# Moving the last batches' comparisons and row additions ahead, and summing both in one loop, in a graph layer kernel

## The reference

```python
h = maximum(layernorm(x), 0)
ea = edge_attr @ W_edge.T + b_edge
msg = relu(h[src] + ea)                                 # one row of 96 for each edge
aggr = segment_sum(msg, dst, num_segments=6250)
z = relu(((1 + eps) * h + aggr) @ W1.T + b1)
return x + z @ W2.T + b2
```

## Time and profile before

| | |
|---|---|
| median of the runs | 1079.86 us |
| span of the profiled execution | 1239.1 us |
| PE busy | 628.9 us, 51% |
| DVE busy | 518.5 us, 42% |
| ACT busy | 193.0 us, 16% |
| POOL busy | 785.9 us, 63% |
| chain that ended last | 56% another core or an unknown queue, 23% DVE, 8% issue, 8% DVE's queue, 3% PE |

### The profile page before, as it was taken

One profiled execution on the slowest core, in us unless ns is written; L12 is line 12 of the kernel. 1 busy time (PEld: TensorE's weight loads), 2 busy tenths in 40 slices (PEclk: granted clock), 3 DMA queues, 4 the chain that ended last, 5 costly groups with the idle time before them and its releaser, 6 DMA issues.

```text
span 1239.1 us, 9124 instructions
## 1 busy us (share of the span) xinstructions
PE 628.9 (51%) x2786; PEld 515.6 (42%) x2786; DVE 518.5 (42%) x658; ACT 193.0 (16%) x233; POOL 785.9 (63%) x838
## 2 busy tenths in 40 slices
PE   2226544455554454555554555444555545554568
PEld 2215434344433334444444444343444434443456
DVE  6645344444433333354344333333343444333373
ACT  5102111111111111111111111111111111111114
POOL 6756666666666666666666666666666666666540
PEclk9999666665656665565665656655556565565668
DMA  8513222333222223333333332222222333232212
GB/s 217 145 33 94 66 64 67 74 85 74 67 67 67 68 67 75 72 73 75 74 93 95 76 74 66 67 67 67 64 66 68 74 88 72 68 67 61 49 29 78
DMA packets 51183, 93.30 MB, mean 75 GB/s; under 512 B 17722, under 2 KB 20443, under 8 KB 51136
## 3 DMA queue, kind: packets, MB, share of 16 engines
q0 software_dynamic: 26592, 40.85, 16.3%
q1 hardware_dynamic: 24390, 51.63, 15.2%
q10 hardware_dynamic: 154, 0.24, 0.1%
HBM read 87.85 MB, written 4.80 MB: 75 GB/s over the span
## 4 chain that ended last, share of the span: by engine, by line
another core or an unknown queue 56%; DVE 23%; issue 8%; DVEq 8%; PE 3%; DMA 1%; ACT 0%; SPq 0%; ACTq 0%
DVE edge_ps L854 7%; DVE edge_ps L865 5%; DVE msg_parts L879 4%; DVEq L768 3%; DVE acc L759 2%; DVEq L770 2%; DVE acc L849 1%; PE edge_ps L601 1%; DVEq L762 1%; DVE stats L639 1%; PE edge_ps L462 1%; DVEq L795 1%; DVE select L705 1%; DVEq L783 1%
## 5 line engine op out<-in xcount | busy, mean ns | idle before, releaser
L352 POOL DMA_INDIRECT gathered<-h_table,src_all x810 | 764.5, 944 | 396.4 <-issue 234.7
L462 PE MATMUL edge_ps<-w_edge,edge_in 97*128 97x96 f32 x1660 | 403.6, 392 | 521.4 <-issue 517.1
L462 PEld LDWEIGHTS edge_ps<-w_edge,edge_in 97*128 97x128 f32 x1660 | 361.8, 302 | 565.0 <-issue 564.1
L787 DVE TENSOR_REDUCE sums<-agg_ps 128x192 f32<-128x576 f32 x41 | 31.0, 757 | 590.4 <-remote 590.4
L424 ACT ACTIVATE msg_parts<-edge_ps 128x960 bf16<-128x960 f32 (+1 forms) x83 | 79.2, 957 | 970.1 <-DVE edge_ps L865 704.4
L543 PE MATMUL agg_ps<-msg_parts,select 128*128 128x288 bf16 x816 | 167.9, 386 | 6.4 <-issue 6.4
L705 DVE TENSOR_TENSOR select<-const_ps,dst_rel 128x2560 bf16<-128x2560 f32 (+1 forms) x43 | 120.8, 2812 | 34.8 <-issue 28.5
L543 PEld LDWEIGHTS agg_ps<-msg_parts,select 128*128 128x128 bf16 x816 | 109.4, 134 | 60.9 <-issue 8.1
L865 DVE TENSOR_TENSOR edge_ps<-edge_ps,gathered 128x960 f32<-128x960 f32 (+1 forms) x83 | 90.9, 1141 | 47.9 <-remote 42.8
L854 DVE SCALAR_TENSOR_TENSOR edge_ps<-edge_ps,msg_parts 128x960 f32<-128x960 f32 (+1 forms) x83 | 91.1, 1144 | 0.3 <-issue 0.3
L879 DVE TENSOR_TENSOR msg_parts<-edge_ps,msg_parts 128x960 bf16<-128x960 f32 (+1 forms) x83 | 90.8, 1136 | 0.3 <-issue 0.3
(11 more groups left out here) (73 smaller groups left out, 143.1 us busy)
## 6 DMA issues: line engine op xcount, KB each, us to landing
edge_in<-edge_t_dram SPq DMA_DIRECT2D x165, 240.0 KB
gathered<-h_table,src_all POOLq DMA_INDIRECT x810
x_all<-x_dram SPq DMA_DIRECT2D x5, 420.0 KB
h_all<-x_dram SPq DMA_DIRECT2D x10, 210.0 KB
out_dram<-h_all SPq DMA_DIRECT2D x10, 210.0 KB
h_table<-h_all SPq DMA_DIRECT2D x3, 420.0 KB
h_table<-h_all SPq DMA_DIRECT2D x1, 630.0 KB
dst_by_row<-dst_rows_dram SPq DMA_DIRECT2D x1, 480.0 KB, 4.2
```

What stands on the lines that cost most here:

```text
L352: nc.gpsimd.indirect_dma_start(out=gathered[c % SLOTS][:, at:at + D], out_offset=None, in_=table, in_offset=bass.IndirectOffsetOnAxis(ap=s ...
L462: mm = pe.matmul(edge_bank(c, g)[:, (k - k0) * D:(k - k0 + 1) * D], edge_in[c % SLOTS][:, k * EDGE_TILE:(k + 1) * EDGE_TILE], w_edge[:], s ...
```

## The change

Late comparisons: both `make_late_select` calls move from behind the loop over batches into its last pass (`c == END`), ahead of the sums of the batch before `END`, with the loads of `END`'s bounds. Row additions: `add_rows(LAST)` moves ahead of `sum_windows(END)` on DVE, so both late row additions stand ahead of it. On PE, the edge features of `LAST` move ahead of the window of `END`. The late sums of both batches are made in one loop, whose length is the larger of their spans (a third small reduction in the set-up makes it). The turn of `END`'s sums and its addition into `acc` come last on both engines.

```diff
--- before.py
+++ after.py
...
@@ -524,17 +524,18 @@
                     pe.reg_add(window, window, 1)
                     pe.reg_add(selects, window, 1)
 
-            def sum_late_windows(c):
-                span = pe.value_load(bounds_i[0:1, 2 * BOUND_ROWS + c:2 * BOUND_ROWS + c + 1], min_val=0, max_val=N - 1)
-                pe.wait_ge(late_relu_done, c - LATE + 1)
-                if c == LAST:
-                    pe.wait_ge(tail_relu_done, 1)
+            def sum_late_windows():
+                span = pe.value_load(bounds_i[0:1, 2 * BOUND_ROWS + JOINT:2 * BOUND_ROWS + JOINT + 1], min_val=0, max_val=N - 1)
                 with pe.Fori(0, span + 1, WINDOW):
-                    this_select = pe.snap(late[c])
-                    pe.wait_ge(late_selected[c], this_select)
-                    sum_rows(c).then_inc(late_summed, 1)
-                    pe.reg_add(window, window, 1)
-                    pe.reg_add(late[c], late[c], 1)
+                    this_select = pe.snap(late)
+                    for c in (LATE, LAST):
+                        pe.wait_ge(late_relu_done, c - LATE + 1)
+                        if c == LAST:
+                            pe.wait_ge(tail_relu_done, 1)
+                        pe.wait_ge(late_selected[c], this_select)
+                        sum_rows(c).then_inc(late_summed, 1)
+                    pe.reg_add(window, window, 2)
+                    pe.reg_add(late, late, 1)
 
             def sum_parts(c):
                 for s in range(SIDES):
@@ -559,23 +560,25 @@
             for c in range(BATCHES):
                 if 0 <= c - BASE_FROM < BASES:
                     turn_base(c - BASE_FROM)
-                if c == LAST:
+                if c == LATE:
+                    edge_features(LAST)
+                    sum_windows(END)
+                elif c == LAST:
                     turned_window = pe.snap(window)
+                    sum_late_windows()
                     pe.wait_ge(sums_made, turned_window)
                     pe.wait_ge(acc_summed, turned_window)
                     turn_sums().then_inc(agg_done, 1)
                     pe.reg_add(window, window, 1)
-                    sum_late_windows(LATE)
-                elif c >= 1:
-                    sum_windows(c - 1)
-                if c + 1 < BATCHES:
+                else:
+                    if c >= 1:
+                        sum_windows(c - 1)
                     if c == 0:
                         pe.wait_ge(ones_copied, 1)
                     edge_features(c + 1)
-            sum_late_windows(LAST)
             all_summed = pe.snap(window)
             all_selects = pe.snap(selects)
-            all_late = {c: pe.snap(late[c]) for c in (LATE, LAST)}
+            all_late = pe.snap(late)
 
             def hidden_sums(c):
                 if c >= 2:
...
@@ -716,6 +719,8 @@
                                                 bounds_f[0:1, 0:BOUND_ROWS], ALU.subtract))
                 sides_of = span_f[:, 0:BOUND_ROWS].rearrange("p (c s) -> p c s", s=SIDES)
                 ordered(nc.vector.tensor_reduce(span_f[:, BOUND_ROWS:BOUND_ROWS + BOUND_ROWS // 2], sides_of, AX.X, ALU.max))
+                ordered(nc.vector.tensor_reduce(span_f[:, BOUND_ROWS + JOINT:BOUND_ROWS + JOINT + 1],
+                                                span_f[:, BOUND_ROWS + LATE:BOUND_ROWS + LAST + 1], AX.X, ALU.max))
                 nc.vector.tensor_copy(bounds_i[:, 2 * BOUND_ROWS:2 * BOUND_ROWS + BOUND_ROWS // 2],
                                       span_f[:, BOUND_ROWS:BOUND_ROWS + BOUND_ROWS // 2]).then_inc(bounds_ready, 1)
 
@@ -764,11 +769,15 @@
                 dve.reg_mul(node[s], node[s], below)
                 dve.reg_add(node[s], node[s], N)
 
+            def load_firsts(c):
+                return [dve.value_load(bounds_i[0:1, SIDES * c + s:SIDES * c + s + 1], min_val=0, max_val=N - 1)
+                        for s in range(SIDES)]
+
+            def load_span(c):
+                return dve.value_load(bounds_i[0:1, 2 * BOUND_ROWS + c:2 * BOUND_ROWS + c + 1], min_val=0, max_val=N - 1)
+
             def load_bounds(c):
-                firsts = [dve.value_load(bounds_i[0:1, SIDES * c + s:SIDES * c + s + 1], min_val=0, max_val=N - 1)
-                          for s in range(SIDES)]
-                span = dve.value_load(bounds_i[0:1, 2 * BOUND_ROWS + c:2 * BOUND_ROWS + c + 1], min_val=0, max_val=N - 1)
-                return firsts, span
+                return load_firsts(c), load_span(c)
 
             def lower_offsets(at, tiles):
                 return nc.vector.tensor_scalar(dst_rel[:, at:at + tiles], dst_rel[:, at:at + tiles], float(-WINDOW), None,
@@ -808,31 +817,31 @@
                     dst_rel[:, first_tile[c]:first_tile[c] + tiles].unsqueeze(2).broadcast_to((128, tiles, WINDOW)),
                     ALU.is_equal).then_inc(late_selected[c], 1)
 
-            def sum_late_windows(c, firsts, span):
-                at, tiles = first_tile[c], tiles_of[c] + (c == LAST)
+            def sum_late_windows(firsts, span):
                 with dve.Fori(0, span + 1, WINDOW) as done:
-                    this_window, this_late = dve.snap(window), dve.snap(late)
-                    dve.reg_add(window, window, 1)
-                    dve.reg_add(offsets, offsets, 1)
-                    dve.reg_add(late, late, 1)
-                    next_window, lowered = dve.snap(window), dve.snap(offsets)
-                    for s in range(SIDES):
-                        next_node(s, firsts[s], done)
-                    cols = [cols_of(s) for s in range(SIDES)]
-                    dve.wait_ge(late_summed, this_late)
-                    dve.wait_ge(acc_summed, this_window)
-                    add_sums(0, cols[0], late_sums(c, 0)).then_inc(side_summed, 1)
-                    lower_offsets(at, tiles).then_inc(offsets_made, 1)
-                    dve.wait_ge(side_summed, this_window)
-                    add_sums(1, cols[1], late_sums(c, 1)).then_inc(acc_summed, 1)
+                    for c in (LATE, LAST):
+                        this_window, this_late = dve.snap(window), dve.snap(late)
+                        dve.reg_add(window, window, 1)
+                        dve.reg_add(offsets, offsets, 1)
+                        dve.reg_add(late, late, 1)
+                        for s in range(SIDES):
+                            next_node(s, firsts[c][s], done)
+                        cols = [cols_of(s) for s in range(SIDES)]
+                        dve.wait_ge(late_summed, this_late)
+                        dve.wait_ge(acc_summed, this_window)
+                        add_sums(0, cols[0], late_sums(c, 0)).then_inc(side_summed, 1)
+                        lower_offsets(first_tile[c], tiles_of[c] + (c == LAST)).then_inc(offsets_made, 1)
+                        dve.wait_ge(side_summed, this_window)
+                        add_sums(1, cols[1], late_sums(c, 1)).then_inc(acc_summed, 1)
+                    lowered, next_window = dve.snap(offsets), dve.snap(window)
                     dve.wait_ge(offsets_made, lowered)
                     dve.wait_ge(acc_summed, next_window)
-                    make_late_select(c)
-
-            def add_turned():
+                    for c in (LATE, LAST):
+                        make_late_select(c)
+
+            def add_turned(turned, cols):
                 this_window = dve.snap(window)
-                cols = [cols_of(s) for s in range(SIDES)]
-                dve.wait_ge(agg_done, this_window)
+                dve.wait_ge(agg_done, turned)
                 dve.wait_ge(acc_summed, this_window)
                 add_sums(0, cols[0], turned_of(0)).then_inc(side_summed, 1)
                 dve.wait_ge(side_summed, this_window)
@@ -890,6 +899,10 @@
                     dve.wait_ge(tail_edge_done, 1)
                     dve.wait_ge(tail_gather_in, 16)
                     nc.vector.tensor_tensor(tail_gathered[:], tail_ps, tail_gathered[:], ALU.add).then_inc(tail_added, 1)
+                if c == END:
+                    make_late_select(LATE)
+                    make_late_select(LAST)
+                    end_bounds, joint_span = load_bounds(END), load_span(JOINT)
                 if c >= 1:
                     if 0 < c - BASE_FROM <= BASES:
                         dve.wait_ge(base_put, c - BASE_FROM)
@@ -903,15 +916,13 @@
                     dve.wait_ge(h_by_act, ACT_PARTS)
                     dve.wait_ge(h_by_dve, DVE_PARTS)
                     nc.vector.memset(hidden[D:D + 1, :], 1.0).then_inc(hidden_ones_set, 1)
-            make_late_select(LATE)
-            make_late_select(LAST)
-            end_bounds, late_bounds, last_bounds = (load_bounds(c) for c in (END, LATE, LAST))
             add_rows(LATE)
+            add_rows(LAST)
             sum_windows(END, *end_bounds)
-            add_rows(LAST)
-            add_turned()
-            sum_late_windows(LATE, *late_bounds)
-            sum_late_windows(LAST, *last_bounds)
```

(14 more changed lines are left out.)

## The result

The changed kernel took 1088.16 us (median of 5, 1087.33 to 1088.60), the kernel before 1079.23 us (5 runs): a ratio of 1.0077, 95% interval 1.0066 to 1.0088. In a later set of its own it was 1.0070 (1.0057 to 1.0084). The forecast was 1084.7 us, 4.8 us slower, with 1087.3 as the upper end: the direction is right, and the time lies 0.9 us above the range.

The account below looks back on a forecast made before the run. The pace of POOL's gathers, 1.25 us each, was taken as the bound. The MLP start moves from G + L + 6.8 to G + L + 11.6: 4.8 us on the median 1079.86 gives 1084.7 us, range 1078.3 to 1087.3.

Parts of the forecast that it names:

- Timed runs don't have the late PE of the profile: Steady part: POOL hardly waits in timed runs, so 161.8 us of its profiled waits go, leaving a span of 1077.3 us.
- The 8.0 us that this left over: Whole kernel: median less 1071.9 us (profiled span without POOL's waits and 5.4 us of end), around the span or unaccounted for.
- G: End of the last gather's issue on POOL, 1196.41 us in the prediction's profile; the end's times count from it.
- first rival: Kernel's end: PE's answers late in timed runs too; changed kernel 0.5 us faster, 1079.3 us; chance 0.25.
- The chain behind `LAST`'s add: DVE's end in the changed kernel: from `LAST`'s add, waiting for the very last gather, to the MLP, 11.6 us.
- Late compares ahead are free: DVE before `END-1`'s sums: two compares, 2.21 us, moved ahead cost nothing and gain nothing, as the next stop is a landing.
- The end of before: Kernel before, last gather's issue end to the MLP: G + L + 6.8, against G + L + 11.6 after the change.
- L: Time from the end of a gather's issue to its data being usable, taken as 2.0 us, ends 1.7 and 4.2.
- L stands once in both figures and drops out: MLP start in both kernels: each figure holds L once, so it leaves the difference of 4.8 us.
- Clock: MLP's first block on PE: a longer PE gap may lower its clock, 2.2 us more, 1086.9 us; chance 0.07.
- G is the same in both: Last gather's issue: the change doesn't delay it; taken as nothing.
- the set-up's delay: Set-up on DVE: the added joint-bound reduction could delay the end, bounds nothing and 1.4 us, taken as nothing.

Follow-up runs that it names:

- r1_before: The kernel before, unchanged, run again for a profile in which POOL doesn't wait: ratio 0.9999 to the kernel before beside it.
- r17_reduce: The kernel before with only the small set-up reduction added, its result not read, where POOL doesn't wait: ratio 0.9998 to the kernel before.
- r11_best: Changed kernel reordered: compares and all loads ahead of `END`'s row additions, `LAST`'s add behind `END`'s sums, turn ahead of the joint loop: 1.0006 to the kernel before.
- r18_best3: r11_best with before's PE order of `END`'s window and `LAST`'s edge features, plus 24 identity products on PE: ratio 1.0004 to the kernel before.

## Why the mechanism held and the size came out too small

- *Timed runs don't have the late PE of the profile*: right. It was read from the 161.8 us of POOL's waits; in the changed kernel's profile POOL waits for nothing. The 8.0 us that this left over can now be placed. POOL's usual gap of 0.3 us stays where a wait goes: 252.1 us at 827 places in r1_before against 240.2 us at 788, 11.9 us more. The gathers from the table began at 32.0 us instead of 35.8. So G would be 1196.41 - 161.8 + 11.9 - 3.8 = 1042.7, and it was 1042.82 and 1042.67. These 8.1 us are the bulk; a time 1.8 us longer than its span (1079.02 and 1077.2) and the shorter end and MLP, 1.4 and 1.2 us, nearly cancel. That 1077.3 came so near the median, which the prediction counted for its first rival, was chance.
- *The chain behind `LAST`'s add*, forecast 11.6: measured 11.42. Its pieces hold too: 2.8 us of loads and 1.1 of register work, 3.83 us together; 2.07 us for both accumulations to the end of the last (forecast 2.15); compares 2.22; turn 0.69.
- *Late compares ahead are free*: right. `END-1`'s reduction stood at G - 9.08 instead of G - 11.16, and DVE then waited 0.83 us for `LATE`'s rows.
- *The end of before, G + L + 6.8 with L = 2.0, so 8.8*: **this term failed**, the largest miss of the sum. It was 7.51 and 7.19. From `END`'s landing to `LAST`'s add it was 17.9 us, not 18.4; from there to the MLP 5.47 and 5.09, not 5.9, a stretch that I took whole from a profile in which the late sums' 28 matmuls took 5.26 us instead of 4.96 and DVE waited 1.68 us for them instead of 1.25; and `END`'s rows came 1.6 us behind their issue (1026.94 against G - 17.5), not 2.0.
- *L stands once in both figures and drops out*: wrong. They are landings of different gathers. In before it is `END`'s, 1.6 us; in the changed kernel it is the very last one, 2.38 and 2.74 us. Over the nine profiles in which DVE waited for the last gather, its add started 1.51 to 1.60 us behind G in five and 2.38 to 2.88 us in four. In before the last landing was no constraint: 2.5 us from its issue's start in both executions, 1.5 us behind G, and DVE came at 2.04 and 2.10. Whether the change makes a late landing likelier isn't shown; its own two other executions had one late (2.74) and one early (1.56). The Trainium skill, DMA: Bandwidth & Descriptors, "Anatomy of one DMA", has about 2.0 us of fixed cost for a DMA from GpSimd's queue. None of these adds started between 1.60 and 2.38, and the measured times decide.
- *Clock*: it stood as a rival with 2.2 us and a chance of 0.07, and at nothing in the sum. The block at the low level costs 1.9 us or more, but before pays some of it too, so it is 0.4 us of the difference in the mean of the two pairs, which is less than two executions of one kernel differ by.
- *G is the same in both*: this was put at nothing (the set-up's delay had the bounds nothing and 1.4). It was 1.3 us in the means. The reduction doesn't do it (r17_reduce); two executions of the changed kernel differ by 1.0 us themselves, and the cause is open.

Together: to the 4.8 forecast come 1.4 us because before's end is shorter (7.35 in the mean, not 8.8) and 0.6 because the last landing is later (2.56, not 2.0), and 0.2 of the chain go: 6.6 us up to the MLP. Clock 0.4 and G 1.3 are the rest of 8.35. The 6.1 us from the add to the MLP are shown by the runs that undo parts of it; the landing, the clock's share and G, 2.2 us together, rest on two executions of each kernel and aren't shown to belong to the change.

## What to carry to other kernels

An instruction that waits for the last transfer of a kernel must have behind it on its engine only work that needs that transfer. Here 11.4 us stood behind it, and 5.1 to 5.5 in the kernel before; bringing it down to 4.8 and 4.2 (r11_best, r18_best3) gave no gain that the runs can tell from none. When two figures are subtracted, a latency that stands in both drops out only if it is the same transfer's. And a profile whose span is 15% off the times can still carry the forecast, if the waits that make up the difference are found first and the end is rebuilt without them.

## What was not expected of the hardware

The same program takes 1078 or 1238 us, set by set. In the long kind PE's edge-feature matmuls often come one by one, 0.7 or 1.4 us apart (at 601.12, 602.51 and 603.91 us of the first profile, say). DVE's reduction of PE's sums stood idle 590.4 us in 39 places, some 15 us a batch, and the trace couldn't find what ended these waits. What causes the long kind no run here shows. The last gather of 128 rows landed 1.5 to 1.6 or 2.3 to 2.8 us behind its issue's end, from one execution to the next; four of the eleven profiles in which POOL doesn't wait have the late value.
